# A fused attention and feed-forward kernel on one core: GpSimd's clips and VectorE's last additions trade places in the tail, and unread products are put into the start of each second pass

## The reference, cut to what matters

```python
x = x + conv_ref(ln_c(x), Wf, bf, Wv, bv, Wp, bp, alpha, beta)   # attention of tokens over 16 centers, 8 heads
t = tokens(x)
t = t + ffn_ref(ln_t(t), W1, b1, W2, b2)
# attention, on one quarter (28 x 28 = 784 tokens) of one image at a time:
sim  = sigmoid(beta + alpha * cosine(centers, tokens))
mask = one_hot(argmax(sim over centers))        # the first of equal ones
out  = (sim * mask) spread over (aggregated values / sums)
# feed-forward, "bitlinear" twice, in 5 groups of images (32 // 5 = 6 images each):
y = x @ sign(W - mean) + b
q = clip(y * 128 / (max|y| + 1e-5), -128 + 1e-5, 128 - 1e-5)    # max over one group; images 30 and 31: q = 0
# first bitlinear, gelu, second bitlinear
```

## Time and profile before

| what | value |
|---|---|
| median of 3 runs | 3026.89 us (3021.84 to 3042.65) |
| the profiled execution: its own time | 3034.4 us |
| its span, first to last instruction | 3032.6 us |
| busy: PE, DVE, ACT, POOL | 2832.6, 2687.9, 2179.0, 1969.9 us |
| mean granted TensorE clock, share of full speed | 0.984 |

### The profile page before, as it was taken

One profiled execution on the slowest core, in us unless ns is written; L12 is line 12 of the kernel. 1 busy time (PEld: TensorE's weight loads), 2 busy tenths in 40 slices (PEclk: granted clock), 3 DMA queues, 4 the chain that ended last, 5 costly groups with the idle time before them and its releaser, 6 DMA issues.

```text
span 3032.6 us, 62753 instructions
## 1 busy us (share of the span) xinstructions
PE 2832.6 (93%) x20998; PEld 1958.3 (65%) x20998; DVE 2687.9 (89%) x5540; ACT 2179.0 (72%) x4510; POOL 1969.9 (65%) x4275
## 2 busy tenths in 40 slices
PE   3999999999999999999999999999999999999987
PEld 2666676656666665667666556666655676666654
DVE  3788888899999989899999999999989999998975
ACT  1677777887677779677767987777789777767952
POOL 1566666437777753677777777777767777776354
PEclk9999999999999999999999999999999999999997
DMA  1011111002222210122222012222200222221034
GB/s 44 17 40 34 33 33 33 9 17 65 65 65 65 65 49 1 49 65 72 73 66 63 3 34 72 72 66 65 57 25 17 65 65 65 65 65 49 1 92 132
DMA packets 30932, 154.29 MB, mean 51 GB/s; under 512 B 6483, under 2 KB 6804, under 8 KB 30612
## 3 DMA queue, kind: packets, MB, share of 16 engines
q1 hardware_dynamic: 30612, 150.28, 17.7%
HBM read 75.60 MB, written 74.66 MB: 50 GB/s over the span
## 4 chain that ended last, share of the span: by engine, by line
PE 45%; POOL 32%; DVE 10%; issue 9%; ACT 2%; SPq 0%; POOLq 0%; DVEq 0%; DMA 0%; ACTq 0%
PE ps L969 18%; POOL mo_x L384 6%; PE ps L1102 6%; PE ps L1046 6%; PE ps L906 5%; DVE st_x L663 5%; PE ps L925 3%; POOL mo_x L379 3%; DVE cenx L672 3%; PE ps L1029 3%; POOL turns L468 2%; POOL n2c L399 2%; ACT turns L579 1%; PE ps L986 1%; POOL nxy L422 1%
## 5 line engine op out<-in xcount | busy, mean ns | idle before, releaser
L969 PE MATMUL ps<-wfT,xn 97*112 97x384 f32 x1792 | 729.4, 515 | 0.3 <-ACT sq L523 0.2
L1046 PE MATMUL ps<-tok,w1T 98*128 98x392 f16 x2880 | 601.6, 331 | 12.6 <-ACT turns L582 7.8
L523 ACT ACTIVATE sq<-ps 112x384 f32<-112x384 f32 x896 | 431.7, 490 | 224.2 <-PE ps L969 221.6
L468 POOL CAST turns<-turns 128x392 f16<-128x392 f32 x240 | 273.0, 1146 | 251.7 <-ACT turns L579 249.6
L774 DVE TENSOR_REDUCE hmax<-ps 128x1 f32<-128x392 f32 x720 | 383.6, 561 | 49.2 <-PE ps L1046 28.4
L1046 PEld LDWEIGHTS ps<-tok,w1T 98*128 98x128 f16 x2880 | 270.3, 98 | 226.7 <-issue 63.5
L707 DVE TENSOR_REDUCE n<-sq 112x32 f32<-112x1536 f32 (+1 forms) x256 | 396.2, 1548 | 23.2 <-ACT sq L523 9.1
L969 PEld LDWEIGHTS ps<-wfT,xn 97*112 97x112 f32 x1792 | 283.1, 182 | 178.6 <-issue 50.9
L579 ACT ACTIVATE turns<-ps,scale 128x1176 f32<-128x1176 f32 x240 | 339.1, 1413 | 37.3 <-DVE scale L797 35.2
L529 ACT ACTIVATE sig<-cosb,betac 112x896 f32<-112x896 f32 x128 | 133.3, 1041 | 321.0 <-DVE cosb L717 321.0
L492 ACT ACTIVATE xnT<-ps,mo_x 112x96 f32<-112x96 f32 x896 | 305.2, 455 | 70.9 <-POOL mo_x L386 70.9
(11 more groups left out here) (143 smaller groups left out, 6166.7 us busy)
## 6 DMA issues: line engine op xcount, KB each, us to landing
xbuf<-in_x SPq DMA_DIRECT2D x64, 588.0 KB, 4.6
out<-xbuf SPq DMA_DIRECT2D x64, 588.0 KB, 6.0
turns<-out SPq DMA_DIRECT2D x60, 588.0 KB, 6.2
out<-turns SPq DMA_DIRECT2D x60, 588.0 KB, 4.4
tok<-in_L_ffn_W SPq DMA_DIRECT2D x2, 142.5 KB
cst<-in_constants SPq DMA_DIRECT2D x1, 195.0 KB
wf<-in_L_conv_Wf SPq DMA_DIRECT2D x1, 144.0 KB
tok<-in_L_conv_Wv SPq DMA_DIRECT2D x1, 144.0 KB
```

The source lines that it names most:

```text
L468: nc.gpsimd.tensor_copy(ghi[:, k % 3, HT:2 * HT], gel[:, k % 3, HT:2 * HT]).then_inc(b_mid, 1)
L523: nc.scalar.activation(sq[:, t, :], bank(2 + t % 2, TN, D), ACT.Square).then_inc(f_sq, 1)
L969: mm(bank(2 + t % 2, TN, D), xn[:, k % 2, t * TN:(t + 1) * TN], wfT[:, :], start=True, stop=True)\
L1046: ins = mm(dst, w1T[:, c * 128:(c + 1) * 128], tok[:, bass.ds(place, 1), part, s * HT:(s + 1) * HT].rearrange("p a n -> p (a n)"), start=p ...
```

## The change

Three edits. In the last part GpSimd's step `clipped` moves from behind `center_squares` to the end of the slot, behind `marks`. In the last part VectorE's `finish` moves in front of `masked`. In every group, `unread(5)` is issued by TensorE behind the `up` of the second tile of the second pass (tile k = 1 at place 0). The other parts keep their order, and no wait is added or taken away.

```diff
@@ gpsimd
             def attention(g, part):
+                late = [(R, 0, clipped(g, part), FINAL)]
                 return [(X, 1, moments("x", EPS_C)), (M, 1, norm_guess), (M, 1, newton), (M, 1, cubic),
-                         (X, 1, center_squares), (R, 0, clipped(g, part), FINAL), (X, 1, center_norms),
-                        (A, 0, marks), (R, 0, moments("t", EPS_T), FFN)]
+                         (X, 1, center_squares)] + (late if part != "last" else []) + [
+                        (X, 1, center_norms), (A, 0, marks), (R, 0, moments("t", EPS_T), FFN)] + (late if part == "last" else [])
@@ vector
                          (X, 1, q_placed), (M, 0, norms(0, TA)),
-                         (X, 0, stats("x", 0)), (A, 0, masked), (R, 0, finish(part), FINAL)]
+                         (X, 0, stats("x", 0))] + (
+                        [(A, 0, masked), (R, 0, finish(part), FINAL)] if part != "last" else
+                        [(R, 0, finish(part), FINAL), (A, 0, masked)])
@@ tensor
                     for c in range(FC):
                         ins = hidden(bank(3 - 3 * (k % 2) + c, 128, HT), place, k % 2, c)
                     ins.then_inc(bh_ps, 1)
+                    if place == 0 and k == 1:
+                        unread(5)
                     if place == 0 and k == 0:
                         row_to_column(2 * g + 1, 0)
                         done(pe, "q_done", g * GQ + (GQ - 1 + X))
```

## The result

| | before | after |
|---|---|---|
| median | 3025.7 us (4 runs, 3021.84 to 3042.65) | 3052.57 us (4 runs, 3048.92 to 3059.63) |
| the profiled execution, its span | 3034.4, 3032.6 us | 3051.05, 3049.2 us |
| ratio | | 1.0088, 95% interval 1.0067 to 1.0109 |

The change costs 0.9%, outside the forecast's range (3014 to 3047). It explains those 16.6 us and not the other 10.

A forecast was written before the change was run, and what follows sets the result against it. No single engine was taken to bound the kernel (chain of waits: TensorE 45%, GpSimd 32%). 3034.4 - 9.0 (second passes) + 0 + 0.2 (tail) = 3025.6, say 3026 us; own range 3018 to 3033, whole range 3014 to 3047.

The forecast's parts named there:

- What bounds a pass, and the marks of the two rhythms: Second passes: no single engine bounds; GpSimd's 48 casts take 33.9 us in short passes, 85.6 in long; VectorE's cast 365 or 513 ns.
- A float32 product is two passes: Unread products in second passes: five take 2.3 us, fill TensorE's 1.29 us idle, keep its clock full; third gelu at +3.80.
- The nearest row is that of group 0, so I take the short rhythm for all five: Second passes: third gelu timing resembles group 0's, so all five take 105.3 us, 526.5 against 535.5, -9.0 us.
- Rival A: Second passes: GpSimd's cast gets in first at the fifth tile, all five take 109.4 us; 3046 us in all; chance 0.28.
- Tail, clips: Tail: with the clips at the end, TensorE's 1.80 us wait before `q_back` goes in slots 2 and 3, -1.8 each.
- Tail, turned order: Tail, `finish` before `masked`: `summed` comes at +8.1 instead of +6.0, +2.1 less 0.4 free, so +1.7 us a slot.
- The sum of +0.2: Tail, both moves over six slots: +1.7, -0.9, -0.1, +1.4, -3.4, +1.5, together +0.2 us.
- the bounds (+8): Tail: idle stretch of about 3 us ahead of `sim_back`; +8 us if all slots fall to half clock, -6 if fewer do.
- rival C: Tail: the forecast, but TensorE loses its clock in every slot, 3026 + 8 = 3034 us; chance 0.1.
- Slot 5: Tail, fifth slot: the additions fill VectorE's 3.38 us wait for `find_first`, so 3.4 us is won outright.
- Slot 6: Tail, last slot: clips come behind the marks, so `masked` starts at 3019.7 instead of 3018.09, +1.5 us.
- The stretches between passes: Stretches between the second passes, about 448.5 to 450.8 us each: left as they are, 0, bounds -6 and +3.

## Why the prediction was wrong

- **What bounds a pass, and the marks of the two rhythms**: right. GpSimd's 34 or 85 us told them apart in every pass of kernels that keep the order of the casts, and VectorE's cast is 507 ns in the changed kernel's group 2, as the long rhythm's 513 of before.
- **"A float32 product is two passes", 2.3 us for five, the clock stays full, third gelu at +3.80**: right in kind, the gelu is at +3.68 since the ten matmuls take 2.16 from first start to the next matmul (1674.23 to 1676.39).
- **"The nearest row is that of group 0, so I take the short rhythm for all five" (-9.0)**: this step failed. It was +12.3. The quantity compared, the distance of the third gelu from the first, does not decide; seven products put it at +4.54 and the passes stayed long. The trace of before already spoke against it: in group 4 the third gelu is 3.21 behind the first, as in group 2, and its pass is short. What parts the two groups is the fifth tile, where in group 4 VectorE's cast is ahead by 0.03:

```profile
2790.61 1.24 ACT L579 ACTIVATE turns<-ps,scale 128x1176 f32<-128x1176 f32 x1 [6.70 <-DVE scale L797]
...
2793.82 1.26 ACT L579 ACTIVATE turns<-ps,scale 128x1176 f32<-128x1176 f32 x1
...
2800.15 0.37 DVE L837 CAST turns<-turns 128x392 f16<-128x392 f32 x1 [0.15 <-ACT turns L579]
...
2800.18 0.71 POOL L468 CAST turns<-turns 128x392 f16<-128x392 f32 x1 [1.69 <-ACT turns L579]
```

Rival A had the mechanism and the number: the fourth gelu 1.60 later instead of 1.70, GpSimd ahead by 0.07 (measured 0.06), 547.0 us for the five (547.8). It had been given 0.28, though on its own scale the 0.07 lay close to group 2's 0.09 (GpSimd wins) and far from group 0's -0.02. The choice between ends was made on the wrong scale. The Trainium skill's rule ("SBUF — State Buffer", section "Who interferes with whom"), that who issues first keeps the shared ports, stood with A. The trace agrees at this tile in four kernels (VectorE ahead by 0.02 to 0.03: 0.35 to 0.36 us; behind by 0.06 to 0.09: 0.67). It does not agree where GpSimd's cast meets the long instruction: there it took 1.97 us though it was 0.23 ahead.
- **Tail, clips (-1.8 in slots 2 and 3)**: sign right, size off: a full-clock slot wins 1.0. VectorE still waits 0.95 for `q_back`, and there the features became the pace.
- **Tail, turned order (+1.7 a slot)**: right in size at full clock, 1.8 measured (21.9 against 20.1), though about 0.45 of it is the longer additions, which the +1.7 did not have. The sum of +0.2 is the second step that failed: the tail costs +13.0, and it failed on the clock, which was put into the bounds (+8) and rival C instead of the sum. The idle stretch was foreseen at 3 us and is 3.5, and it lowers the clock in each slot; products in it give back 16 us.
- **Slot 5 (-3.4)**: it is 1.9 shorter (21.4 against 23.3), and the reason given does not hold. That slot is 19.6 at full clock with the turned order and 19.0 with the old order and late clips, so it is not the additions in front that win there. Clips and additions ran together in it, and the four clips took 5.42 us instead of 3.92.
- **Slot 6 (+1.5)**: it is 4.3 longer (27.2 against 22.9). Here too clips and additions run together, and the clips take 5.41 us. With the additions moved alone the clips keep their 3.90, the slot is 23.8 and the whole tail 145.8: put together, the two moves in the tail cost 4 us more than the additions alone. How much of this is the clips and how much the clock (0.73 against 0.76 in that slot) is not parted.
- **The stretches between passes (0, down to -6)**: -6.5, just past the bound. The start up to the first gelu (-2.2) was not in the sum. The profiles of the other kernels have the stretches 1.9 to 8.7 shorter than before and the first gelu between 557.8 and 561.5 us, with and without the products; no edit is shown to be the cause.
- **A and C as rivals of each other**: they are about different stages and both came true. Their prices add: 3034.4 + 11.5 + 8 + 0.2 = 3054, and the profiled execution took 3051.05. That it comes so near is in part luck: the tail cost 13.0 and not 8.2, and the stretches and the start gave back 8.7 that no sum had. The range was built as if only one of the two could come true.

## What to carry to other kernels

When a repeated stage has two lengths in one trace, find the first tile at which they part and compare the change on the quantity that parts them, not on a delay that lies before it; then a filler of a few tenths of a microsecond can choose the rhythm for good. A step moved in front of another on one engine should be priced also by the idle stretch it makes on TensorE, since what follows the stretch may run at half clock, and that was the larger part of the cost here. Rivals in different stages are not alternatives: let the range reach to their sum.

## What the runs showed of the hardware

- Two casts that VectorE and GpSimd start within 0.1 us of each other: with VectorE 0.03 ahead 0.36 and 0.71 us; with GpSimd 0.06 to 0.09 ahead 0.67 and 0.51 to 0.55 us.
- A GpSimd cast that starts inside VectorE's long instruction (1.37 us) can take 2.8 to 3.2 us, longer than any instruction of VectorE beside it. In group 2 of the changed kernel the casts take 3.05 to 3.21 and 0.64 us by turns from the eighth tile on: the one that starts 0.57 into a long instruction (at 1710.55) ends 0.37 behind the end of the next long one. That it is passed over more than once is my reading; no run shows it by itself.
- Seven float32 products of 256 columns in a 3.5 us idle stretch kept TensorE at full clock in four slots in a row, where without them each slot was at 0.75 to 0.86.
